# Per-head weight products of an attention kernel as 64-row tiled matmuls instead of zero-padded 128-row ones

## The chip, the cores and the metric

The kernel runs on one NeuronCore of one Trainium2 chip. The metric is device time in microseconds of one execution. The kernel before takes 453.39 us, the median of three runs (453.31 to 454.78).

## The reference, cut to what matters

Four sub-layers follow each other on x of shape (8, 256, 128), each added to its input: an attention with a time-difference kernel, a gated feed-forward layer, a causal softmax attention with 16 heads of 64, and the same feed-forward layer again. The change touches only what the third one prepares from its weights:

```
q = einsum('bsd,hda->bhsa', residual, Wq) + bq
k = einsum('bsd,hda->bhsa', residual, Wk) + bk
v = einsum('bsd,hda->bhsa', residual, Wv) + bv
scores = einsum('bhsa,bhta->bhst', q, k) * 64 ** -0.5
pattern = softmax(where(causal, scores, -1e5))
out = einsum('bsha,had->bsd', einsum('bhst,bhta->bhsa', pattern, v), Wo) + bo
```

The kernel does not form q and k. For each head it forms the 128x128 product of Wq and Wk once, and the 128x128 product of Wv and Wo once, and works with these. Each of the 32 products (16 heads, two kinds) contracts over the 64 elements of a head. The biases give a vector per head (Wk times bq) and one vector for the output (Wo times bv, summed over the heads, plus bo).

## The kernel before, in words

The rows of x are worked on in four pairs of batches (512 rows, 4 tiles of 128). A prologue brings the first pair through the first attention and the first feed-forward layer, and prepares all weights. Then a loop of 4 x 32 steps runs the softmax attention, one head and one batch a step, and the other layers of the neighbouring pairs are laid between its steps. An epilogue ends the last pair.

The order is written out by hand in the list PROLOGUE (lines 61 to 69) as triples of a job, a first tile and a count of tiles. Every engine walks the same list and does its part of each job, so each engine's queue has the order of the list and the engines wait for each other by semaphores. The jobs in the prologue are: lns0 and lns1 (layer norm on VectorE, with the power on GpSimd), lntA, lntF and lntB (transposes on TensorE, then a rounded copy xt_hi or rt_hi on ScalarE and the rest xt_lo or rt_lo on VectorE), qkv0 to qkv2, mean, vwo, mat0, mat1 and aout (the first attention), gu0 to gu2 and down (feed-forward), w0 to w7 (weight products) and wb (biases). The jobs before the loop share two PSUM banks, X and Y; a job that writes one waits until the reader before has finished (the counters x_free and y_free).

The weights lie in SBUF with two heads above each other: partitions 0 to 63 hold an even head, 64 to 127 the odd one. To contract over 64 rows with 128-row matmuls, the kernel before keeps wv1, wq1 and bq1 with both heads' columns side by side and zeros in the half that belongs to the other head. The zeros are written by VectorE (line 611) and GpSimd (lines 759, 760), and the loads of Wv (ScalarE's queue, line 488) and of Wq and bq (SyncE's queue, lines 262, 263) wait for them.

A weight job w0 to w7 (lines 378 to 391) makes four heads' products in one PSUM bank, u_ps for even and v_ps for odd job numbers. These two banks are free until the loop. TensorE runs 4 fp32 matmuls, which are 8 weight loads and 8 matmul instructions; ScalarE copies the whole bank (128x512) into the rounded part wvo_hi or m_hi (line 546); VectorE forms the rest wvo_lo or m_lo (line 718). Job wi waits for the VectorE part of job w(i-2). The job wb (lines 370 to 377) has 8 matmuls of wk against two columns of bq1 and 8 of wo against one column of bv, and ScalarE copies both results.

The first work of the loop is u_proj and v_proj (line 283 to 285 through split3), which need all of m_hi, m_lo, the first wvo_hi and wvo_lo, and rt_hi and rt_lo of lntB.

Of the kernel before, what the change touches and what calls it, by code (L numbers as in the profile page):

```python
# [21 lines left out]
P = 128  # L22
ALU = mybir.AluOpType
ACT = mybir.ActivationFunctionType
F32 = mybir.dt.float32
# [10 lines left out]
STEPS = 2 * H  # L36
GH = PAIR // D
# [44 lines left out]
WEIGHTS = [f"w{i}" for i in range(8)]  # L82
# [46 lines left out]
def build(nc, x_d, wa_d, ga_d, woa_d, boa_d, wq_d, wk_d, wv_d, wo_d, bq_d, bv_d, bo_d, wg_d, wu_d, wd_d, out_d):  # L129
# [3 lines left out]
    with ExitStack() as ctx:  # L133
# [14 lines left out]
        wq1, wv1, bq1 = sb("wq1", [P, H // 2, 2, D]), sb("wv1", [P, H // 2, 2, D]), sb("bq1", [P, 2, H // 2])  # L148
# [34 lines left out]

        u_tiles = u_ps[:].rearrange("p (b t q) -> p b t q", b=2, t=2)
# [3 lines left out]
        zeros_v, zeros_q = sem("zeros_v"), sem("zeros_q")  # L188
# [60 lines left out]
        def _(sp):  # L249
# [9 lines left out]
            sp.wait_ge(zeros_q, 2)  # L259
            for i in range(2):  # L260
                half = slice(i * A, (i + 1) * A)
                sp.dma_start(wq1[half, :, i, :], wq_d[half, :, :]).then_inc(ld_q, 16)
                sp.dma_start(bq1[half, i, :], bq_d[half, :]).then_inc(ld_q, 16)
            sp.dma_start(bv[:], bv_d).then_inc(ld_q, 16)
            sp.dma_start(bo[:], bo_d).then_inc(ld_q, 16)
# [15 lines left out]
        def _(pe):  # L281
# [15 lines left out]
            def side(job, t0, nt, at):  # L297
# [72 lines left out]
                elif job == "wb":  # L370

                    pe.wait_ge(w_lo, 8)
                    for i in range(H // 2):
                        nc.tensor.matmul(v_ps[:, 2 * i:2 * i + 2], wk[:, i, :], bq1[:, :, i], start=True, stop=True)
                    for i in range(H // 2):
                        last = nc.tensor.matmul(v_ps[:, H:H + 1], wo[:, i, :], bv[:, i:i + 1], start=(i == 0), stop=(i == H // 2 - 1))
                    last.then_inc(w_full, 1)
                elif job in WEIGHTS:

                    i = int(job[1])  # L380
                    if i == 0:
                        pe.wait_ge(ld_v, 16 * 3)
                    if i == 4:
                        pe.wait_ge(ld_q, 16 * 7)
                    if i >= 2:
                        pe.wait_ge(w_lo, i - 1)
                    left, right = (wv1, wo) if i < 4 else (wq1, wk)
                    for j in range(4):
                        h = 4 * (i % 4) + j
                        last = nc.tensor.matmul((u_ps, v_ps)[i % 2][:, j * D:(j + 1) * D], left[:, h // 2, h % 2, :], right[:, h // 2, :], start=True, stop=True)  # L390
                    last.then_inc(w_full, 1)
# [89 lines left out]
        def _(act):  # L481
            act.dma_start(wo[:], wo_d).then_inc(ld_v, 16)
            act.wait_ge(consts_in, 4)
            nc.scalar.activation(warm[:], minus_half[:, 0:1], ACT.Tanh)
            act.wait_ge(zeros_v, 1)
            for i in range(2):
                half = slice(i * A, (i + 1) * A)
                act.dma_start(wv1[half, :, i, :], wv_d[half, :, :]).then_inc(ld_v, 16)

            def side(job, t0, nt, at):  # L490
# [47 lines left out]
                elif job == "wb":  # L538
                    act.wait_ge(w_full, 9)
# [70 lines left out]
        def _(dve):  # L610
            nc.vector.memset(wv1[:], 0.0).then_inc(zeros_v, 1)

# [6 lines left out]
            def side(job, t0, nt, at):  # L619
# [93 lines left out]
                elif job in WEIGHTS:  # L713
                    i = int(job[1])
                    dve.wait_ge(w_hi, i + 1)
                    hs = slice(4 * (i % 4), 4 * (i % 4) + 4)
                    hi, lo = ((wvo_hi, wvo_lo), (m_hi, m_lo))[i // 4]
                    nc.vector.scalar_tensor_tensor(lo[:, hs, :], (u_ps, v_ps)[i % 2][:].rearrange("p (j d) -> p j d", d=D),
                                                   (1.0, SCORE_SCALE)[i // 4], hi[:, hs, :].bitcast(F32), ALU.mult, ALU.subtract).then_inc(w_lo, 1)
# [34 lines left out]
        def _(pool):  # L754
# [4 lines left out]
            nc.gpsimd.memset(bq1[:], 0.0).then_inc(zeros_q, 1)  # L759
            nc.gpsimd.memset(wq1[:], 0.0).then_inc(zeros_q, 1)  # L760
# [66 lines left out]
```

## Time and profile before

| what | us |
|---|---|
| median of three runs | 453.39 |
| lowest, highest | 453.31, 454.78 |
| span of the profiled execution | 451.1 |
| TensorE matmul busy in the span | 405.4 (90%) |
| ScalarE busy | 310.5 (69%) |
| VectorE busy | 307.7 (68%) |
| first matmul of the loop (u_proj) starts at | 58.33 |

The span runs from the first to the last recorded instruction of the one profiled execution. That execution's own time is not given beside it; the median of the runs is 2.3 us above the span. Times inside the span are counted from its start. PE is TensorE's matmuls and PEld its weight loads, DVE VectorE, ACT ScalarE, POOL GpSimd and SP SyncE; PEq and ACTq stand for what an engine's own sequencer issues. A matmul's busy time includes the time until its result is out, so matmuls that follow each other overlap in the record.

### The profile page before, as it was taken

How to read it: one execution, taken by the hardware profiler on the slowest of the kernel's cores; microseconds unless marked ns; L12 is line 12 of the kernel's file. 1: busy time of each engine (PE TensorE's matmuls, PEld its weight loads, DVE VectorE, ACT ScalarE, POOL GpSimd, SP SyncE). 2: the span in 40 equal slices, each digit the busy share in tenths (PEclk: the TensorE clock that was granted, in tenths of full speed). 3: DMA queues.
4: the chain of work that ended last, by engine and by line, in shares of the span. 5: the costliest groups of instructions: out<-in, count | busy, mean ns of one | idle time of the engine just before them, and what ended most of it. 6: DMA issues, size and time to landing. Idle time of an engine off the chain costs nothing.

```text
span 451.1 us, 8672 instructions
## 1 busy us (share of the span) xinstructions
PE 405.4 (90%) x2591; PEld 359.2 (80%) x2591; DVE 307.7 (68%) x1322; ACT 310.5 (69%) x945; POOL 34.1 (8%) x48
## 2 busy tenths in 40 slices
PE   0857688999999999999999999999999999999766
PEld 0756677878889988888899889888899898999545
DVE  4465538666878776977777858886786687766542
ACT  1443158797868897976768887876688888778420
POOL 4030100100000000200000002000000000000000
PEclk9998869999999999999999999999999999999955
DMA  8600000000000000000000000000000000000000
GB/s 221 140 1 1 1 1 1 1 1 1 2 0 2 1 1 2 1 1 11 15 1 1 1 1 1 1 1 24 2 0 2 2 0 2 2 23 2 1 1 23
DMA packets 8157, 5.68 MB, mean 13 GB/s; under 512 B 944, under 2 KB 7856, under 8 KB 8112
## 3 DMA queue, kind: packets, MB, share of 16 engines
q1 hardware_dynamic: 6912, 4.08, 3.7%
q10 hardware_dynamic: 1200, 1.05, 0.8%
q8 instruction: 22, 0.36, 0.3%
q14 instruction: 23, 0.19, 0.1%
HBM read 4.08 MB, written 1.05 MB: 11 GB/s over the span
## 4 chain that ended last, share of the span: by engine, by line
PE 75%; ACT 10%; DVE 7%; issue 4%; DMA 2%; POOL 0%; ACTq 0%; DVEq 0%
PE bank L452 11%; PE bank L283 9%; PE bank L284 9%; PE bank L285 9%; PE bank L437 9%; PE bank L361 6%; PE bank L454 5%; PE bank L427 5%; PE bank L390 2%; DVE gated L698 2%; ACT prob L571 2%; PE bank L351 2%; DMA wv<-wv_in 2%; PE bank L306 2%; ACT gate_t L537 1%
## 5 line engine op out<-in xcount | busy, mean ns | idle before, releaser
L579 ACT ACTIVATE prob_t<-bank 128x384 f32<-128x384 f32 x128 | 62.8, 490 | 22.7 <-PE bank L437 22.5
L452 PE MATMUL bank<-prob_t,v 128*128 128x256 f32 x256 | 76.5, 381 | 0.7 <-ACT o_t L604 0.7
L437 PE MATMUL bank<-ident,prob 128*128 128x128 f32 x384 | 63.8, 275 | 4.7 <-ACT prob_t L579 4.6
L571 ACT ACTIVATE prob<-neg_s,neg_max 128x256 f32<-128x256 f32 x128 | 64.3, 503 | 0.0
L569 ACT ACTIVATE prob<-neg_s,neg_max 128x128 f32<-128x128 f32 x128 | 51.5, 403 | 12.3 <-DVE neg_max L737 12.0
L735 DVE CUSTOM_DVE_ANT_0 neg_s<-bank,mask 128x128 f32<-128x128 f32 x128 | 36.7, 287 | 33.8 <-PE bank L285 33.8
L437 PEld LDWEIGHTS bank<-ident,prob 128*128 128x128 f32 x384 | 45.4, 140 | 15.1 <-DVE prob L746 5.0
L454 PEld LDWEIGHTS bank<-prob_t,v 128*128 128x128 f32 x256 | 48.5, 190 | 6.7
L737 DVE CUSTOM_DVE_ANT_0 neg_s<-bank,mask 128x256 f32<-128x256 f32 x128 | 53.7, 420 | 0.0
L427 PE MATMUL bank<-rt,u 128*128 128x128 f32 x256 | 49.8, 276 | 0.8 <-DVE neg_max L737 0.8
L454 PE MATMUL bank<-prob_t,v 128*128 128x128 f32 x256 | 49.1, 274 | 0.0
L452 PEld LDWEIGHTS bank<-prob_t,v 128*128 128x128 f32 x256 | 42.9, 190 | 7.2 <-issue 1.9
L553 ACT ACTIVATE u<-bank,u_bias 128x256 f32<-128x256 f32 x64 | 30.1, 470 | 25.6 <-PE bank L285 25.5
L283 PE MATMUL bank<-rt_hi,u_hi 128*128 128x256 f32 x128 | 46.7, 364 | 0.0
L746 DVE TENSOR_SCALAR prob<-prob,row_inv 128x256 f32<-128x256 f32 x128 | 45.5, 355 | 0.0
L561 ACT ACTIVATE v<-bank 128x512 f32<-128x512 f32 x64 | 38.3, 598 | 10.1 <-PE bank L285 9.3
L427 PEld LDWEIGHTS bank<-rt,u 128*128 128x128 f32 x256 | 41.1, 192 | 3.6 <-issue 1.0
L772 POOL TENSOR_TENSOR rstd<-var,minus_half 128x4 f32<-128x4 f32 (+1 forms) x20 | 17.8, 888 | 313.4 <-DVE var L636 313.4
L745 DVE TENSOR_SCALAR prob<-prob,row_inv 128x128 f32<-128x128 f32 x128 | 37.5, 293 | 4.6
L723 DVE SCALAR_TENSOR_TENSOR u_lo<-bank,u_bias,u_hi 128x256 fp32r<-128x256 f32 x64 | 30.8, 481 | 13.6 <-ACT u_hi L554 13.5
L285 PE MATMUL bank<-rt_lo,u_hi 128*128 128x256 f32 x128 | 36.0, 281 | 0.0
L284 PE MATMUL bank<-rt_hi,u_lo 128*128 128x256 f32 x128 | 35.9, 280 | 0.0
(117 smaller groups left out, 879.4 us busy)
## 6 DMA issues: line engine op xcount, KB each, us to landing
x<-x_in SPq DMA_DIRECT2D x3, 256.0 KB, 7.0
out<-x SPq DMA_DIRECT2D x3, 256.0 KB, 2.3
wo<-wo_in ACTq DMA_DIRECT2D x1, 512.0 KB, 4.3
wv<-wv_in ACTq DMA_DIRECT2D x2, 256.0 KB, 6.8
wk<-wk_in SPq DMA_DIRECT2D x1, 512.0 KB, 8.1
wq<-wq_in SPq DMA_DIRECT2D x2, 256.0 KB, 8.6
x<-x_in SPq DMA_DIRECT2D x2, 128.0 KB, 4.3
out<-x SPq DMA_DIRECT2D x2, 128.0 KB, 1.8
```

Of the source, the lines that this page charges most:

```text
L283: nc.tensor.matmul(out, w_hi_ap, r_hi_ap, start=True, stop=False)
L284: nc.tensor.matmul(out, w_lo_ap, r_hi_ap, start=False, stop=False)
L285: return nc.tensor.matmul(out, w_hi_ap, r_lo_ap, start=False, stop=True)
L427: nc.tensor.matmul(S[:, 0:P], u[:, i, b, :], rt[:, q, t:t + P], start=True, stop=True)
L437: last = nc.tensor.transpose(pt_ps[:, j * P:(j + 1) * P], prob[:, k % 4, j * P:(j + 1) * P], ident[:])
L452: nc.tensor.matmul(o_ps[:, b * N:(b + 1) * N], vg[:, 2 * b, hs], prob_t[:, k % 2, 0:N], start=(step == 0), stop=False, skip_group_check=True)
L454: nc.tensor.matmul(o_ps[:, b * N + P:(b + 1) * N], vg[:, 2 * b + 1, hs], prob_t[:, k % 2, N:SC], start=False, stop=(step >= STEPS - 2), sk ...
L569: nc.scalar.activation(prob[:, q, 0:P], neg_s[:, r, 0:P], ACT.Exp, bias=neg_max[:, q, 0:1], scale=-1.0, accum_out=row_sum[:, q, 0:1])
L571: nc.scalar.activation(prob[:, q, P:SC], neg_s[:, r, P:SC], ACT.Exp, bias=neg_max[:, q, 1:2], scale=-1.0, accum_out=row_sum[:, q, 1:2]).th ...
L579: nc.scalar.activation(prob_t[:, k % 2, :], pt_ps[:, 0:SC], ACT.Copy).then_inc(pt_sb, 1)
L737: nc.vector.tensor_tensor_reduce(out=neg_s[:, r, P:SC], in0=s_ps[r][:, P:SC], in1=mask[:], scale=-1.0, scalar=3e38, op0=ALU.add, op1=ALU.m ...
L746: nc.vector.tensor_scalar(prob[:, q, P:SC], prob[:, q, P:SC], row_inv[:, q, 1:2], None, ALU.mult).then_inc(p_norm, 1)
```

## The change: what it does

The products use 64-row slices of the weights, the even head in partitions 0 to 63 and the odd one in 64 to 127. The two go to different PSUM banks: even heads to u_ps, odd heads to v_ps. One job now makes eight heads in both banks, with 8 matmuls of 64 rows (alternating between the halves), two copies on ScalarE and two rests on VectorE. Both of a job's copies wait for its last matmul. There are four such jobs, w0 to w3. The job wb has 16 matmuls of 64 rows and one column for the bq part and two copies of its result. The zero memsets and the waits for them are gone; Wv is issued on ScalarE's queue right behind Wo as one load of 512 KB, Wq as one load of 512 KB.

In the list, w0 stays where it was, and w1, w2 and w3 stand where w2, w4 and w6 stood. The places of the former w1, w3, w5 and w7 are empty.

```diff
+HALVES = (slice(0, A), slice(A, P))
-    ("lntA", 2, 2), ("w1", 0, 0), ("qkv1", 0, 2), ("qkv0", 2, 2), ("qkv1", 2, 2), ("qkv2", 0, 2), ("mean", 0, 2), ("w2", 0, 0),
-    ("vwo", 0, 2), ("qkv2", 2, 2), ("mat0", 0, 2), ("mean", 2, 2), ("mat1", 0, 2), ("w3", 0, 0), ("vwo", 2, 2), ("mat0", 2, 2),
-    ("aout", 0, 2), ("mat1", 2, 2), ("w4", 0, 0), ("lns0", 0, 2), ("lns1", 0, 2), ("aout", 2, 2), ("lns0", 2, 2),
-    ("lntF", 0, 2), ("gu0", 0, 2), ("lns1", 2, 2), ("w5", 0, 0), ("lntF", 2, 2), ("gu0", 2, 2), ("w6", 0, 0), ("gu1", 0, 2),
-    ("w7", 0, 0), ("gu2", 0, 2), ("down", 0, 2), ("lns0", 0, 2), ("gu1", 2, 2), ("gu2", 2, 2), ("down", 2, 2), ("lns0", 2, 2),
+    ("lntA", 2, 2), ("qkv1", 0, 2), ("qkv0", 2, 2), ("qkv1", 2, 2), ("qkv2", 0, 2), ("mean", 0, 2), ("w1", 0, 0),
+    ("vwo", 0, 2), ("qkv2", 2, 2), ("mat0", 0, 2), ("mean", 2, 2), ("mat1", 0, 2), ("vwo", 2, 2), ("mat0", 2, 2),
+    ("aout", 0, 2), ("mat1", 2, 2), ("w2", 0, 0), ("lns0", 0, 2), ("lns1", 0, 2), ("aout", 2, 2), ("lns0", 2, 2),
+    ("lntF", 0, 2), ("gu0", 0, 2), ("lns1", 2, 2), ("lntF", 2, 2), ("gu0", 2, 2), ("w3", 0, 0), ("gu1", 0, 2),
+    ("gu2", 0, 2), ("down", 0, 2), ("lns0", 0, 2), ("gu1", 2, 2), ("gu2", 2, 2), ("down", 2, 2), ("lns0", 2, 2),
...
-            sp.wait_ge(zeros_q, 2)
-            for i in range(2):
-                half = slice(i * A, (i + 1) * A)
-                sp.dma_start(wq1[half, :, i, :], wq_d[half, :, :]).then_inc(ld_q, 16)
-                sp.dma_start(bq1[half, i, :], bq_d[half, :]).then_inc(ld_q, 16)
-            sp.dma_start(bv[:], bv_d).then_inc(ld_q, 16)
-            sp.dma_start(bo[:], bo_d).then_inc(ld_q, 16)
+            for dst, src in ((wq, wq_d), (bq, bq_d), (bv, bv_d), (bo, bo_d)):
+                sp.dma_start(dst[:], src).then_inc(ld_q, 16)
...
-                        nc.tensor.matmul(v_ps[:, 2 * i:2 * i + 2], wk[:, i, :], bq1[:, :, i], start=True, stop=True)
+                        for half, ps in zip(HALVES, w_banks):
+                            nc.tensor.matmul(ps[:, i:i + 1], wk[half, i, :], bq[half, i:i + 1], start=True, stop=True)
...
-                    if i >= 2:
-                        pe.wait_ge(w_lo, i - 1)
-                    left, right = (wv1, wo) if i < 4 else (wq1, wk)
+                    if i:
+                        pe.wait_ge(w_lo, 2 * i)
+                    left, right = (wv, wo) if i < 2 else (wq, wk)
                     for j in range(4):
-                        h = 4 * (i % 4) + j
-                        last = nc.tensor.matmul((u_ps, v_ps)[i % 2][:, j * D:(j + 1) * D], left[:, h // 2, h % 2, :], right[:, h // 2, :], start=True, stop=True)
+                        for half, ps in zip(HALVES, w_banks):
+                            last = nc.tensor.matmul(ps[:, j * D:(j + 1) * D], left[half, 4 * (i % 2) + j, :], right[half, 4 * (i % 2) + j, :],
+                                                    start=True, stop=True)
                     last.then_inc(w_full, 1)
...
             act.dma_start(wo[:], wo_d).then_inc(ld_v, 16)
+            act.dma_start(wv[:], wv_d).then_inc(ld_v, 16)
             act.wait_ge(consts_in, 4)
             nc.scalar.activation(warm[:], minus_half[:, 0:1], ACT.Tanh)
-            act.wait_ge(zeros_v, 1)
-            for i in range(2):
-                half = slice(i * A, (i + 1) * A)
-                act.dma_start(wv1[half, :, i, :], wv_d[half, :, :]).then_inc(ld_v, 16)
...
-                    nc.scalar.activation(u_bias[:], v_ps[:, 0:H], ACT.Copy, scale=SCORE_SCALE)
+                    for e in range(2):
+                        nc.scalar.activation(u_bias[:, e:H:2], w_banks[e][:, 0:H // 2], ACT.Copy, scale=SCORE_SCALE)
...
-                    dst = (wvo_hi, m_hi)[i // 4][:, 4 * (i % 4):4 * (i % 4) + 4, :]
-                    nc.scalar.activation(dst, (u_ps, v_ps)[i % 2][:].rearrange("p (j d) -> p j d", d=D), ACT.Copy,
-                                         scale=(1.0, SCORE_SCALE)[i // 4]).then_inc(w_hi, 1)
+                    for e in range(2):
+                        dst = (wvo_hi, m_hi)[i // 2][:, 8 * (i % 2) + e:8 * (i % 2) + 8:2, :]
+                        nc.scalar.activation(dst, w_banks[e][:].rearrange("p (j d) -> p j d", d=D), ACT.Copy,
+                                             scale=(1.0, SCORE_SCALE)[i // 2]).then_inc(w_hi, 1)
...
-            nc.vector.memset(wv1[:], 0.0).then_inc(zeros_v, 1)
...
-                    dve.wait_ge(w_hi, i + 1)
...
+                    for e in range(2):
+                        dve.wait_ge(w_hi, 2 * i + e + 1)
+                        hs = slice(8 * (i % 2) + e, 8 * (i % 2) + 8, 2)
+                        nc.vector.scalar_tensor_tensor(lo[:, hs, :], w_banks[e][:].rearrange("p (j d) -> p j d", d=D),
+                                                       (1.0, SCORE_SCALE)[i // 2], hi[:, hs, :].bitcast(F32), ALU.mult, ALU.subtract).then_inc(w_lo, 1)
...
-            nc.gpsimd.memset(bq1[:], 0.0).then_inc(zeros_q, 1)
-            nc.gpsimd.memset(wq1[:], 0.0).then_inc(zeros_q, 1)
```

## Rows read from the trace of the kernel before

**Rows 1.** The page: busy us (share) and instructions; granted clock in 40 slices; a group.

```profile
PE 405.4 (90%) x2591; PEld 359.2 (80%) x2591; DVE 307.7 (68%) x1322; ACT 310.5 (69%) x945; POOL 34.1 (8%) x48
...
PEclk9998869999999999999999999999999999999955
...
L437 PE MATMUL bank<-ident,prob 128*128 128x128 f32 x384 | 63.8, 275 | 4.7 <-ACT prob_t L579 4.6
```

**Rows 2.** Windows: stretch, length, busy us (instructions) by engine, PEclk, DMA share, GB/s.

```profile
33.00:36.40 3.40, 2.99 (x14) 2.93 (x14) 1.62 (x5) 0.43 (x2) 0.70 (x1) 0.50 0.02 5
...
58.33:63.80 5.47, 5.47 (x14) 4.36 (x15) 0.48 (x1) 2.03 (x4) 0.00 (x0) 0.50 0.01 3
63.80:440.00 376.20, 359.12 (x2341) 319.29 (x2340) 274.31 (x1223) 290.27 (x900) 22.41 (x23) 0.99 0.01 3
```

**Rows 3.** Chain that ended last, 0 to 110 us: start, length, what.

```profile
3.67 7.50 DMA wv<-wv_in
...
13.29 0.33 PE bank L283
...
50.64 1.68 PE bank L374 x16
```

**Rows 4.** DMA issues of the page: count, KB each, median us to landing.

```profile
wo<-wo_in ACTq DMA_DIRECT2D x1, 512.0 KB, 4.3
wv<-wv_in ACTq DMA_DIRECT2D x2, 256.0 KB, 6.8
```

**Rows 5.** Windows of one us in the load phase.

```profile
3.00:4.00 1.00, 0.00 (x0) 0.00 (x0) 0.00 (x0) 0.00 (x0) 0.68 (x3) 1.00 1.06 421
```

**Rows 6.** Timeline, 3 to 17 us: start, us, engine, line, what, count, idle before.

```profile
3.01 1.29 ACTq L488 DMA_DIRECT2D wv<-wv_in  x2
...
5.23 0.49 DVE L631 BATCH_NORM_STATS2 stats<-x 128x6 f32<-128x128 f32 x2 [2.25 <-DMA x<-x_in]
...
12.50 0.42 DVE L658 TENSOR_TENSOR xt_lo<-bank,xt_hi 128x256 fp32r<-128x256 f32 x1
...
14.27 1.87 PE L390 MATMUL bank<-wo,wv 128*128 128x128 f32 x8
...
15.02 0.42 DVE L658 TENSOR_TENSOR xt_lo<-bank,xt_hi 128x256 fp32r<-128x256 f32 x1 [0.38 <-ACT xt_hi L497]
...
16.17 0.60 ACT L546 ACTIVATE wvo_hi<-bank 128x512 fp32r<-128x512 f32 x1 [1.19 <-PE bank L390]
...
16.67 0.56 ACT L513 ACTIVATE t_qkv<-bank,ga_bias,ga_scale 128x256 f32<-128x256 f32 x1
```

**Rows 7.** Timeline, 19 to 30 us.

```profile
19.97 1.14 PE L390 MATMUL bank<-wo,wv 128*128 128x128 f32 x8
...
24.86 0.62 POOL L786 TENSOR_SCALAR stdp<-signed 128x512 f32<-128x512 f32 x1 [1.13 <-DVE signed L687]
...
25.55 0.97 PEld L341 LDWEIGHTS bank<-vwo,stdp 128*128 128x128 f32 x8 [0.62 <-issue]
...
27.14 0.69 DVE L687 SCALAR_TENSOR_TENSOR signed<-less,expd 128x512 f32<-128x512 f32 x1
...
28.27 0.69 DVE L718 SCALAR_TENSOR_TENSOR m_lo<-bank,m_hi 128x512 fp32r<-128x512 f32 x1 [0.44 <-ACT m_hi L546]
...
28.88 0.48 DVE L631 BATCH_NORM_STATS2 stats<-x 128x6 f32<-128x128 f32 x2
```

**Rows 8.** Timeline, 35 to 44 us.

```profile
35.43 0.60 DVE L642 TENSOR_SCALAR xn<-x,mv,rstd 128x128 f32<-128x128 f32 x2
...
36.98 0.69 DVE L718 SCALAR_TENSOR_TENSOR m_lo<-bank,m_hi 128x512 fp32r<-128x512 f32 x1 [0.96 <-ACT m_hi L546]
37.59 0.41 DVE L658 TENSOR_TENSOR xt_lo<-bank,xt_hi 128x256 fp32r<-128x256 f32 x1
...
40.42 0.69 DVE L718 SCALAR_TENSOR_TENSOR m_lo<-bank,m_hi 128x512 fp32r<-128x512 f32 x1 [0.47 <-ACT m_hi L546]
...
43.59 1.42 PEld L361 LDWEIGHTS bank<-wd,hid 128*128 128x128 f32 x12 [1.35 <-DVE hid L701]
```

**Rows 9.** Timeline, 50 to 55 us.

```profile
50.48 1.84 PE L374 MATMUL bank<-bq,wk 128*128 128x2 f32 x16
...
52.03 0.60 DVE L642 TENSOR_SCALAR xn<-x,mv,rstd 128x128 f32<-128x128 f32 x2
...
54.41 0.67 PE L306 MATMUL bank<-ident,xn 128*128 128x128 f32 x2
```

More of the change, by code:

```diff
@@ L79 @@
 KINDS = {"lntA": "lnt", "lntF": "lnt", "lntB": "lnt", "gu0": "gu", "gu1": "gu", "gu2": "gu"}
-WEIGHTS = [f"w{i}" for i in range(8)]
+WEIGHTS = [f"w{i}" for i in range(4)]
 class Counts:
@@ L147, in build @@
         wk, wo, bv = sb("wk", [P, H // 2, D]), sb("wo", [P, H // 2, D]), sb("bv", [P, H // 2])
-        wq1, wv1, bq1 = sb("wq1", [P, H // 2, 2, D]), sb("wv1", [P, H // 2, 2, D]), sb("bq1", [P, 2, H // 2])
+        wq, wv, bq = sb("wq", [P, H // 2, D]), sb("wv", [P, H // 2, D]), sb("bq", [P, H // 2])
         bo = sb("bo", [P, 1])
@@ L182, in build @@
         s_ps, pt_ps, u_ps, v_ps, o_ps, X, Y = bank[0:2], bank[2], bank[3], bank[4], bank[5], bank[6], bank[7]
+        w_banks = (u_ps, v_ps)
         u_tiles = u_ps[:].rearrange("p (b t q) -> p b t q", b=2, t=2)
         ld_x0, ld_x1, ld_x, ld_o, ld_a, ld_f, ld_v, ld_q = (sem(n) for n in ("ld_x0", "ld_x1", "ld_x", "ld_o", "ld_a", "ld_f", "ld_v", "ld_q"))
-        zeros_v, zeros_q = sem("zeros_v"), sem("zeros_q")
         consts = sem("consts")
@@ L381, in side @@
                     if i == 0:
-                        pe.wait_ge(ld_v, 16 * 3)
-                    if i == 4:
-                        pe.wait_ge(ld_q, 16 * 7)
-                    if i >= 2:
-                        pe.wait_ge(w_lo, i - 1)
-                    left, right = (wv1, wo) if i < 4 else (wq1, wk)
+                        pe.wait_ge(ld_v, 16 * 2)
+                    if i == 2:
+                        pe.wait_ge(ld_q, 16 * 5)
+                    if i:
+                        pe.wait_ge(w_lo, 2 * i)
+                    left, right = (wv, wo) if i < 2 else (wq, wk)
                     for j in range(4):
-                        h = 4 * (i % 4) + j
-                        last = nc.tensor.matmul((u_ps, v_ps)[i % 2][:, j * D:(j + 1) * D], left[:, h // 2, h % 2, :], right[:, h // 2, :], start=True, stop=True)
+                        for half, ps in zip(HALVES, w_banks):
+                            last = nc.tensor.matmul(ps[:, j * D:(j + 1) * D], left[half, 4 * (i % 2) + j, :], right[half, 4 * (i % 2) + j, :],
+                                                    start=True, stop=True)
                     last.then_inc(w_full, 1)
@@ L538, in side @@
                 elif job == "wb":
-                    act.wait_ge(w_full, 9)
-                    nc.scalar.activation(u_bias[:], v_ps[:, 0:H], ACT.Copy, scale=SCORE_SCALE)
+                    act.wait_ge(w_full, 5)
+                    for e in range(2):
+                        nc.scalar.activation(u_bias[:, e:H:2], w_banks[e][:, 0:H // 2], ACT.Copy, scale=SCORE_SCALE)
                     nc.scalar.activation(o_bias[:], v_ps[:, H:H + 1], ACT.Identity, bias=bo[:]).then_inc(w_hi, 1)
@@ L714, in side @@
                     i = int(job[1])
-                    dve.wait_ge(w_hi, i + 1)
[L716 to L719, printed above, removed]
+                    hi, lo = ((wvo_hi, wvo_lo), (m_hi, m_lo))[i // 2]
+                    for e in range(2):
[3 more added lines that the diff above has]
+                                                       (1.0, SCORE_SCALE)[i // 2], hi[:, hs, :].bitcast(F32), ALU.mult, ALU.subtract).then_inc(w_lo, 1)
             def u_low(h):
```

## The prediction

> **What bounds the kernel now.** I read the page first, then windows of busy time, then the chain of waits of the first 110 us, then the timeline of the prologue. The page has TensorE busy for 90% of the span [rows 1]. The windows split this: from 63.8 to 440 us TensorE is busy 359 of 376 us, so the loop is bound by TensorE, and no line of it is in the diff [rows 2]. The change can act only by moving the moment at which the loop starts, 58.33 us, and through the clock that TensorE has there. The prologue is not bound by one engine. It is one chain that passes between VectorE, GpSimd, ScalarE and TensorE, and each weight job lies across it in the three queues.
>
> The clock matters as a second thing. The granted clock is at its lower level (0.50, which is 1.2 GHz) from about 33 to 36.4 us and again for the first 5.47 us of the loop [rows 2]. At the lower level a weight job of 8 instructions takes 1.87 us, at the upper one 1.14 us [rows 6, 7]. From the starts of these, instructions follow each other by about 0.21 and 0.12 us: 1.14 us less the 0.275 us of one 128-column matmul [rows 1] is spread over 7 intervals.
>
> **The start.** The chain of waits has 7.5 us of the load of Wv in it [rows 3], and the change issues that load at about 1.2 us in place of 3.01 [rows 6]. That looks like a gain of 1.8 us or more, but two queues join at this point. The first real matmul after w0, of qkv0, needs xt_lo, which VectorE ends at 12.50 + 0.42 = 12.92 us [rows 6]; the chain shows TensorE free of w0 at 13.29 us [rows 3]. So the wait for Wv costs only 13.29 - 12.92 = 0.37 us less a hand-over of about 0.1, say 0.25. VectorE's own chain begins at 5.23 us when the first x tiles land [rows 6] and has no long wait after that, so it moves with this landing.
>
> Here the change works against itself. x (128 KB) and Wo (512 KB, landed 4.3 us after issue at 0.7) share the 16 DMA engines, which are full at 3 to 4 us with 421 GB/s [rows 4, 5]. Before, Wv came to the engines only after that. Now it is queued directly behind Wo and keeps the engines full while the last pieces of x move. The upper bound for the delay of x is the whole of Wv at that rate, 512 KB / 421 GB/s = 1.25 us, the lower bound zero. I take a third, +0.4 us, since the two queues share and x is nearly through. The Wq load and the memsets on GpSimd have nothing waiting for them before 26 us; they count zero. So w0 itself leaves the path: -0.25 against +0.4, which is +0.15.
>
> **The former w1.** It ran 14.27 to 16.14 us, while xt_lo of the second half was ready at 15.44 [rows 6]. Without it qkv1 starts about 0.3 us earlier. Then ScalarE's copy for w1 (start to next start 0.50 us) stood ahead of the tanh at 16.67 [rows 6]. Together about -0.45 us, up to -0.7. Against that, w0 and w1 kept TensorE dense from 11 to 16 us, and the durations fall from the slow to the fast kind after w1. Without w1 TensorE is used in pieces there and may stay at the lower level for some us more. Three projections in the chain would each take 0.2 to 0.3 us longer: 0 to +0.7, I take +0.2.
>
> **The new w1 to w3.** Each has 16 loads and 16 matmuls of 64 rows where the job at that place had 8 of 128. The trace has no 64-row matmul. If even and odd halves run fully beside each other, a job takes as long as before, 1.14 us; if not at all, twice as many intervals of 0.12 us, +1.0 us. I take the first, because the two halves use different rows of the array, different partitions and different banks, and keep the second for the range. What is certain is the second copy and the second rest. ScalarE's second copy delays what stands behind it by 0.48 us (0.50 in [rows 6]).
>
> At w1 the chain goes on through ScalarE: vwo, tanh, dist, expd, then signed, stdp and aout. That aout waits for stdp, and not for the former w3, is seen in its weight load at 25.55 us, 0.07 after stdp ends at 24.86 + 0.62 = 25.48 [rows 7]. So w1 costs +0.48, and the removed w3 gives nothing: it was hidden behind this chain.
>
> At w2 (formerly w4) the next link is VectorE's layer norm: m_lo at 28.27, then stats at 28.88, 0.61 us apart [rows 7]. The second rest puts another +0.61 in front of stats. TensorE and VectorE before it, aout, its addition and signed at 27.14 [rows 7], shift as a whole.
>
> The former w5 stood ahead of lntF of the second half. xn was ready at 35.43 + 0.60 = 36.03 us, about when w5 ended, so its TensorE time was hidden, but its rest at 36.98 pushed xt_lo to 37.59 [rows 8]. Without it xt_lo follows ScalarE's copy at about 37.1: -0.47.
>
> The former w6 and w7 become w3. Before, w6's rest at 40.42 and w7's each stood ahead of one feed-forward step, up to down's weights at 43.59 [rows 8]. Now both rests stand ahead of gu1 and none ahead of gu2. Following it with the same durations (copies 0.48 apart, rests 0.61 apart, second half of the job's rest ends near 41.75 instead of 41.1, then gated, hid, gate, gated, hid) down starts at about 43.9: +0.3.
>
> **wb.** xn is ready at 52.03 + 0.60 = 52.63, but lntB starts at 54.41 [rows 9], so wb is on the path. Its bq part has 16 instructions of 0.105 us in the chain, 1.68 us [rows 3]; it gets 32. With halves side by side this stays 1.68, without it grows by 1.68. The second copy of the bias is short and mostly beside lntB's transposes: +0.1.
>
> **Switching.** Going from 128-row to 64-row matmuls may not be pipelined: the matmul before has to leave the array, 0.275 - 0.12 = 0.16 us more than the usual interval [rows 1, 7]. On the path are the entries of w1, w2, w3 and wb and the exit of wb, five, so 0 to 0.8; I take 0.5. The Trainium skill (TensorEngine Tiling (Array Packing), Tiling Modes, Key Properties) says that changing the tiling mode drains TensorE; by it the term is the full 0.8, and no row here shows it. The same section says that tiles can execute weight loads and matmuls in parallel, which speaks for no growth of the jobs; no row shows that either.
>
> **The sum.** 0.15 - 0.45 + 0.2 + 0.48 + 0.61 - 0.47 + 0.3 + 0.1 + 0.5 = +1.4 us at the first u_proj. Two clock terms remain. Around 34 us the former w5 filled TensorE at the lower level (2.99 of 3.40 us busy [rows 2]) and the clock rose right behind it. Without it the clock may rise later, over gu0, w3 and gu1: 0 to +1.3, I take +0.3. At the loop's entry TensorE runs dense at the lower level for 5.47 us. Work there counts half, so a later start inside it loses less: down to -1.0, and if the clock rises later too, up to +1.5; I take -0.1. That is +1.6 us on the span of 451.1, thus 452.7; the median of the runs is 2.3 us above the span, so 453.4 + 1.6 = 455.0 us.
>
> **Rivals.**
> Halves not side by side. For it: before, weight loads alone already set the pace, since the wb matmuls of 2 columns follow each other by 0.105 us, nearly the 0.12 us of those with 128 [rows 3, 7]; if the loads of both halves pass one after the other, nothing overlaps and padding was free. Against it: different rows. Price: three jobs by +0.95 and wb by +1.68, 4.5 us, on top of the 1.6, less about 0.6 for the later entry into the slow stretch: 458.9 us. An overlap in part lies between.
>
> Clock comes up before the loop's dense part, the case on the faster side. The place is the stretch from wb to 63.8 us. Its 5.47 us at the lower level would take 2.7 at the upper one [rows 2], and transposes and the wo part of wb another 0.6. If the shifted work leaves TensorE fast there, 3.3 us come back: +1.6 - 3.3 = -1.7, 451.7 us. It decides once the lower level lasts less than 2.5 us of dense loop work (half of 5.47 - 2.5, about 1.5 us, is then saved). For it: the three runs of one kernel differ by 1.4 us, as a moved clock change would make them. Against it: the change takes TensorE work out of the prologue, and wb keeps its matmuls of one column, behind which the clock fell.
>
> That the change does not do what it says, the padding gone but all costs hidden, is the part of my own case that ends near 453.4.
>
> **How the numbers follow.** No change is what lies within 0.3%, 1.36 us, of 453.39. My case has 0.48: by its own bounds 452.9 to 457.0, of which I give 0.26 slower, 0.20 same, 0.02 faster. Halves one after the other, wholly or in part, 0.34: 0.33 slower, 0.01 same. The clock case 0.18: 0.13 faster, 0.05 same. That makes 0.15 faster, 0.26 same, 0.59 slower. The range goes from the clock case's 451.9 to 459.4, just past the second case.
>
> **What would show it.** Right: u_proj's first matmul at about 59.7 to 60 us; stats of x at about 5.6; qkv0 without a wait for Wv and w0 over long before it; each w1 to w3 about 1.1 to 1.3 us on TensorE at the upper level; two copies 0.48 apart behind each. Wrong: 16 matmuls of a job in over 1.8 us at the upper level (second case); x landing at 5.2 and a chain that does not stretch behind w2 (then my sum is too high by 1); a granted clock of 1.00 before the loop's fifth microsecond. Loop work from 64 to 440 us that changes by more than its shift would say the reasoning misses something altogether.

## The result and the profile after

The changed kernel takes 465.64 us (median of 4 runs, 464.09 to 468.05) against 454.08 us for the kernel before beside it: ratio 1.0243, 95% interval [1.0188, 1.0298]. It is 11.6 us slower. The direction was forecast, the size was not: 455.0 us, range to 459.4. Here and below the ratios are taken from fast runs alone, and four of the ten runs of e9 (462.4 to 462.9 us) are left out of its numbers as slow ones.

The experiments ran in four groups, each beside runs of the kernel before (453.9 to 454.7 us). Where two experiments are compared, the intervals of their ratios say whether the difference is more than noise.

The page of the changed kernel (its first row and the granted clock in 40 slices, as in [rows 1]) and four windows of it (columns as in [rows 2]):

```profile
PE 413.5 (89%) x2607; PEld 364.7 (79%) x2607; DVE 306.0 (66%) x1321; ACT 310.9 (67%) x946; POOL 32.5 (7%) x46
...
PEclk9975658999999999999999999999999999999955
```

```profile
25.80:32.70 6.90, 6.06 (x32) 5.35 (x32) 3.23 (x8) 2.63 (x6) 1.93 (x3) 0.52 0.01 2
...
36.00:46.40 10.40, 6.24 (x30) 4.86 (x30) 4.56 (x13) 2.51 (x6) 0.70 (x1) 0.52 0.00 1
...
49.70:69.20 19.50, 14.96 (x79) 13.09 (x78) 6.31 (x22) 2.48 (x9) 1.43 (x2) 0.50 0.00 1
...
73.30:451.40 378.10, 360.61 (x2346) 320.21 (x2344) 274.49 (x1224) 291.18 (x901) 22.37 (x23) 0.98 0.01 3
```

The loop starts at 69.20 us instead of 58.33, 10.87 us later, and from there to the end of its span of 462.3 us the changed kernel needs 393.1 us, against 392.8 us before, which is the same. So the loss lies ahead of the loop. There the granted clock is at its lower level (0.50, 1.2 GHz) in three long stretches, about 36 us of the time from 25.8 to 69.2. Before, it was low from 33 to 36.4 us [rows 2] and from 53.5 us on (0.50 up to the loop's start), together 8.2 us ahead of the loop.

What this did to the chain of waits is seen by putting its pieces beside each other (start, length, what). The kernel before:

```profile
25.59 1.12 PE bank L341 x8
26.71 0.91 PE bank L390 x8
...
43.60 1.62 PE bank L361 x12
...
49.04 1.60 PE bank L361 x12
50.64 1.68 PE bank L374 x16
52.33 2.22 PE bank L376 x16
```

The changed kernel (L337 is aout, L387 the weight jobs w1, w2, w3, L357 down, L371 and L373 the two parts of wb):

```profile
20.44 1.12 PE bank L387 x16
...
26.48 2.05 PE bank L337 x8
28.53 2.03 PE bank L387 x16
...
42.52 2.03 PE bank L387 x16
...
48.76 2.30 PE bank L357 x12
...
55.48 2.93 PE bank L357 x12
58.41 3.51 PE bank L371 x32
61.91 3.50 PE bank L373 x16
```

aout is +0.93 us, w2 and w3 +1.12 each (the jobs at their places took 0.91 before), the two downs +0.68 and +1.33, wb +1.83 and +1.28: 8.3 of the 10.87 us. Four of these seven pieces have the same instructions as before. A weight job of 16 instructions takes 1.12 us at w1, at the upper level, and 2.03 at w2: the halves do run beside each other, and the clock made the difference. For wb the same is seen in e15 below, where its 32 instructions of 64 rows took 1.95 us at the upper level, against 3.51 here.

The single steps, in the timeline of the changed kernel:

```profile
5.10 0.49 DVE L626 BATCH_NORM_STATS2 stats<-x 128x6 f32<-128x128 f32 x2 [5.10 <-DMA x<-x_in]
...
8.25 2.08 PE L387 MATMUL bank<-wo,wv 64*128 64x128 f32 x16
...
20.37 1.16 PE L387 MATMUL bank<-wo,wv 64*128 64x128 f32 x16
...
28.46 1.79 PEld L387 LDWEIGHTS bank<-wk,wq 64*128 64x128 f32 x16 [0.22 <-issue]
...
31.22 1.29 DVE L714 SCALAR_TENSOR_TENSOR m_lo<-bank,m_hi 128x512 fp32r<-128x512 f32 x2 [1.63 <-ACT m_hi L543]
...
32.42 0.47 DVE L626 BATCH_NORM_STATS2 stats<-x 128x6 f32<-128x128 f32 x2
...
40.75 0.42 DVE L653 TENSOR_TENSOR xt_lo<-bank,xt_hi 128x256 fp32r<-128x256 f32 x1 [1.20 <-ACT xt_hi L492]
```

x lands at 5.10 us (5.23 before [rows 6]); w0 is over at 10.3, long before qkv0. The 16 instructions of w1 take 1.16 us as the 8 did [rows 7]. Rests to stats is now 1.20 us (31.22 to 32.42), 0.61 before [rows 7]. Ahead of the weight loads of w2 there is 0.22 us of idle time that waits for nothing; between gu0 and w5 of the kernel before, at the same level, there is none.

One caution in reading PEclk: it says 1.00 from the start of both kernels, but w0 takes 2.08 us there, the duration of the lower level. The half-job kernel e4 below shows 1.00 up to its loop too, while all its weight jobs last as long as at the lower level. So the column can't be trusted ahead of its first change, and the durations have to be read instead.

Read this way, the first rise came later as well. The projections (qkv0 to qkv2) fall to the shorter duration at 16.1 us in the kernel before; in the changed kernel they still have the longer one at 18.3 us:

```profile
16.10 0.28 PE L284 MATMUL bank<-xt_hi,wa_lo 128*128 128x256 f32 x1
```

```profile
18.06 0.41 PE L280 MATMUL bank<-xt_hi,wa_lo 128*128 128x256 f32 x1
18.27 0.41 PE L281 MATMUL bank<-xt_lo,wa_hi 128*128 128x256 f32 x1
```

### The profile page after: what moved, and what is told of

It reads as the page before. It is cut to its first block, busy times and chain, and to the rows that moved or that the text cites. A ratio compares the mean times of both kernels' runs of the same rounds, so it can differ in the third digit from the quotient of the medians.

```text
span 462.3 us, 8699 instructions
## 1 busy us (share of the span) xinstructions
PE 413.5 (89%) x2607; PEld 364.7 (79%) x2607; DVE 306.0 (66%) x1321; ACT 310.9 (67%) x946; POOL 32.5 (7%) x46
## 4 chain that ended last, share of the span: by engine, by line
PE 73%; ACT 10%; DVE 9%; issue 5%; DMA 1%; POOL 1%; ACTq 0%; DVEq 0%
PE bank L450 10%; PE bank L279 9%; PE bank L280 9%; PE bank L281 9%; PE bank L435 8%; PE bank L357 6%; PE bank L452 5%; PE bank L425 5%; DVE gated L693 2%; PE bank L347 2%; ACT prob L568 2%; PE bank L302 2%; ACT gate_t L532 2%; PE bank L337 2%; PE bank L387 1%
## 5 line engine op out<-in xcount | busy, mean ns | idle before, releaser
L425 PE MATMUL bank<-rt,u 128*128 128x128 f32 x256 | 49.7, 276 | 0.8 <-DVE neg_max L733 0.8
L741 DVE TENSOR_SCALAR prob<-prob,row_inv 128x128 f32<-128x128 f32 x128 | 38.6, 301 | 4.6
```

The lines of the kernel that those rows point to most:

```text
L425: nc.tensor.matmul(S[:, 0:P], u[:, i, b, :], rt[:, q, t:t + P], start=True, stop=True)
```

## The experiments

**Fill the empty places.** The changed kernel with TensorE work added where w1, w3, w5 and w7 stood (e1: all four places, 128 rows; e2: the same with 64-row pairs; e8: only w1's; e14: only the last three).

```diff
+                elif job == "F":
+                    for j in range(4):
+                        nc.tensor.matmul(o_ps[:, j * D:(j + 1) * D], wo[:, j, :], wo[:, j + 4, :], start=True, stop=True)
```

> The changed kernel with four idle 128-row fp32 matmuls (Wo against Wo, into a bank free until the loop, result unused) at each of the four places in the order where w1, w3, w5 and w7 stood before. Theory 1 (the change took TensorE work out of the gaps, so the granted clock fell): the clock stays at 1.00 over most of 16 to 53 us as before, u_proj starts at 58.5 to 61 us instead of 69.2, time 453.5 to 457. Theory 2 (the 64-row matmuls themselves let the clock fall): the low stretches from 26 us stay, time 462 to 467. Theory 3 (the doubled copies and rests behind each job cost it): nothing gained, and the fillers' own 1 to 2 us each come on top, 465 to 470.

Measured 458.99 us, ratio 1.0096 [1.0056, 1.0136]. More work for TensorE, 6.6 us less time. It is 2 us above what theory 1 named, so theory 1 is not the whole. In the profiled execution (456.4 us) u_proj starts at 61.40 us.

```diff
+                        for half, ps in zip(HALVES, (o_ps, s_ps[0])):
+                            nc.tensor.matmul(ps[:, j * D:(j + 1) * D], wo[half, j, :], wo[half, j + 4, :], start=True, stop=True)
```

> As the run with 128-row fillers, but each filler is eight 64-row matmuls, the two halves alternating into two banks, of the same length on TensorE (16 instructions). Theory 1: any dense TensorE work holds the clock, same time as with the 128-row fillers within 1 us, 453.5 to 457. Theory 2: 64-row matmuls count for less, the clock stays low as in the changed kernel, 463 to 468, at least 5 us over the 128-row fillers. Theory 3: as theory 1 of no help, 465 to 470.

Measured 460.62 us, 1.0114 [1.0080, 1.0148]: between the ranges of theories 1 and 2, and not told apart from the 128-row fillers. Pairs of 64 rows hold the clock too; whether quite as well is not shown.

> The changed kernel with the 128-row filler only where the former w1 stood. Of the about 6 us that four fillers brought (465.6 to 459.0), this tells the share of the first rise of the clock. If the fall at 26 us and the later ones come from the other three gaps: 462 to 466. If the first rise decides what follows: 457 to 461.

Measured 465.28 us, 1.0225 [1.0163, 1.0286]: nothing gained, as the first case named (462 to 466). Its profile adds something: with this one filler the clock did not fall at 25.8 us, though w3's place was still empty. It fell at 34.7 us instead and then stayed at 0.50 to 72 us, which cost as much.

> The changed kernel with 128-row fillers at the places of the former w3, w5 and w7, none at w1. With e8_fill_w1_only, which brought nothing: the three places carry the gain, 457 to 461. If it takes all four together, since the first rise comes late without w1: 462 to 466.

Measured 461.01 us, 1.0144 [1.0107, 1.0180]: at the edge of the first range (457 to 461). The three places carry 4.6 of the 6.6 us, though the interval overlaps that of all four. The profiled execution also has the late first rise that the second case named: by the durations TensorE was at the lower level until about 29.5 us, and PEclk says 1.00 there. With a filler at w1's place as well (e1) the rise is at 16.3 us. Below are e14's filler at w3's place, at the lower level, and its first aout, at the upper one:

```profile
27.69 2.06 PE L377 MATMUL bank<-wo 128*128 128x128 f32 x8
...
30.39 1.10 PE L337 MATMUL bank<-vwo,stdp 128*128 128x128 f32 x8
```

In e1's profiled execution the clock stayed at 1.00 where it had first fallen in the changed kernel (25.8 us) and from 44 to 57 us, but it was low from 33.3 to 43.5 us all the same, and again from 57 us:

```profile
26.00:36.00 10.00, 4.98 (x39) 4.33 (x40) 5.62 (x19) 3.38 (x8) 2.83 (x5) 0.86 0.01 2
36.00:46.00 10.00, 8.38 (x47) 6.96 (x45) 4.96 (x12) 2.52 (x7) 0.00 (x0) 0.63 0.00 0
46.00:56.00 10.00, 7.23 (x69) 6.34 (x69) 5.41 (x21) 0.77 (x2) 1.43 (x2) 1.00 0.01 2
```

**Take TensorE work out of the kernel before**, and nothing else (e13).

```diff
-                    for j in range(4):
+                    for j in range(1 if i in (3, 5, 7) else 4):
```

> The kernel before with one matmul of four in each of w3, w5 and w7; 9 of the 32 products are not computed, all copies, rests and waits stay. TensorE has 18 instruction pairs less and nothing else changes. Clock theory: less work is slower, the clock falls near 26 us and is low more often, 457 to 464. Latency theory: up to 0.7 us a job saved where it is on the path, w5 and w7, 451.5 to 453.5.

Measured 458.96 us, 1.0118 [1.0075, 1.0162]: less work, 4.6 us slower. The order, the copies, the rests and the waits are those of the kernel before, and only 9 of the 32 products are left out. So this shows the mechanism without any part of the change. In the profiled execution the loop starts at 62.45 us instead of 58.33 and takes 393.4 us from there. One detail of the expectation missed: the clock fell at about 31 us and not near 26. First the windows of the kernel before, then those of this one, with two of its thinned jobs:

```profile
36.00:46.00 10.00, 6.77 (x46) 5.53 (x46) 5.49 (x14) 3.11 (x7) 0.00 (x0) 0.98 0.00 0
46.00:56.00 10.00, 7.45 (x54) 6.48 (x53) 4.93 (x19) 1.76 (x6) 1.43 (x2) 0.88 0.00 1
```

```profile
36.00:46.00 10.00, 7.06 (x36) 6.12 (x36) 4.75 (x12) 2.62 (x6) 0.00 (x0) 0.73 0.01 2
46.00:56.00 10.00, 8.38 (x41) 7.81 (x40) 4.81 (x19) 0.77 (x2) 1.43 (x2) 0.61 0.00 1
```

```profile
22.91 0.47 PE L390 MATMUL bank<-wo,wv 128*128 128x128 f32 x2
...
33.76 0.63 PE L390 MATMUL bank<-wk,wq 128*128 128x128 f32 x2
```

The granted clock is lower (0.73 and 0.61 against 0.98 and 0.88), and TensorE is busier with fewer instructions.

**Order apart from tiling.** e3: the padded 128-row matmuls of the kernel before, in the changed order (four jobs of eight heads).

```diff
+                    for e in range(2):
+                        for j in range(4):
+                            h = 8 * (i % 2) + 4 * e + j
+                            last = nc.tensor.matmul((u_ps, v_ps)[e][:, j * D:(j + 1) * D], left[:, h // 2, h % 2, :], right[:, h // 2, :], start=True, stop=True)
```

> The kernel before with its padded 128-row matmuls and memsets, but in the changed kernel's order: four jobs of eight heads, each 8 matmuls of 128 rows into both banks, then two copies and two rests. TensorE work is that of before, only lumped. Theory 1: the gaps at the four empty places remain, but each job is twice as long (about 2 us), so the clock falls in part: 456 to 463. Theory 2: with 128-row work the clock holds as before; the lumping alone costs the 1 to 2 us of my prediction plus 3 us of longer jobs, 456 to 459. Theory 3: all of the change's cost is the lumping, 464 or more.

Measured 470.42 us, 1.0331 [1.0271, 1.0391], worse than theories 1 and 2 allowed and within what theory 3 named. The new order costs 16 us with padded matmuls, and tiling takes 4.8 of them away: a merged job took 3.62 us at the lower level, against 2.03 tiled. Lumping alone, with all TensorE work kept, brings the fall (at about 27 us). So the amount of TensorE work alone doesn't decide; where it stands counts as well. The longer jobs also cost by themselves: 1.59 us each at the lower level, 4.8 us for the three behind w0, which is as much as tiling saves in this order.

```profile
45.78 3.62 PE L391 MATMUL bank<-wk,wq 128*128 128x128 f32 x16
```

**How much of the array works.** e4: eight jobs at the old places, each four 64-row matmuls of one half. e7: the same with the other half of the rows busy beside each.

```diff
+                    e, g = i % 2, i // 2 % 2
+                    half = HALVES[e]
+                    for j in range(4):
+                        last = nc.tensor.matmul(w_banks[e][:, j * D:(j + 1) * D], left[half, 4 * g + j, :], right[half, 4 * g + j, :],
+                                                start=True, stop=True)
```

> The kernel before's order with eight jobs, one copy and one rest each, but each job is four 64-row matmuls of one half only (even heads into u_ps, odd heads into v_ps), without padding or memsets, and wb as in the changed kernel. Instructions, job lengths and places are those of before. Theory 1: the clock holds as before, 452 to 455. Theory 2: 64-row work counts for less and the clock falls, 458 to 466. Theory 3: nothing is doubled, 452 to 455.

Measured 470.99 us, 1.0327 [1.0262, 1.0392], 5 us above the highest range named.

```diff
+                        nc.tensor.matmul((o_ps, s_ps[0])[e][:, j * D:(j + 1) * D], left[HALVES[1 - e], 4 * g + j, :], right[HALVES[1 - e], 4 * g + j, :],
+                                         start=True, stop=True)
```

> The half-job kernel (eight jobs of four 64-row matmuls of one half, 471 us) with each matmul preceded by one in the other half of the rows into a bank free until the loop, result unused. The halves overlap, so job lengths stay 2.07 us at the lower clock. Theory R (what holds the clock is how much of the array works, 64 rows alone count for half): the clock rises about 16 to 20 us as in the kernel before, 454 to 459. Theory G (the clock was low because w0 now runs alone at 8 us and leaves a gap up to 12.8 us, rows do not matter): the clock stays low, 466 to 472.

Measured 460.06 us, 1.0128 [1.0049, 1.0207]: eleven us faster by adding matmuls. First a job of the half kernel (the third of eight, all eight took 2.07 us), then two matmuls of the other, from the two halves:

```profile
21.96 2.07 PE L388 MATMUL bank<-wo,wv 64*128 64x128 f32 x8
```

```profile
26.04 0.37 PE L388 MATMUL bank<-wo,wv 64*128 64x128 f32 x1
26.05 0.37 PE L390 MATMUL bank<-wo,wv 64*128 64x128 f32 x1
```

They start 0.01 us apart, so the halves are truly beside each other. In the half kernel's profile no job ever had the shorter duration; by the durations its clock came up only inside the loop. In the other the projections have the shorter duration from 18.0 us. That is what theory R said, though 460.06 us lies just above its range: 64 rows working alone hold the clock much worse than both halves together. The added matmuls double the number of instructions as well as the rows at work, and the two are not told apart by this pair alone; the kernel before, with 128 rows and no more instructions than e4, held the clock.

**No lumping.** e9: tiled pairs in eight small jobs at the old places, half as long on TensorE. e10: every pair computed twice.

```diff
+                    for j in range(2):
+                        for e, half in enumerate(HALVES):
+                            last = nc.tensor.matmul(w_sets[i % 2][e][:, j * D:(j + 1) * D], left[half, 2 * (i % 4) + j, :], right[half, 2 * (i % 4) + j, :],
                                                     start=True, stop=True)
```

> The change without its lumping: 64-row pairs in both halves, no padding or memsets, but eight jobs at the places of the kernel before, each two pairs into two banks (a second set of banks free until the loop alternates), two copies and two rests of 128x256 instead of one of 128x512. TensorE's job is half as long as before (8 instructions, about 0.6 us at the upper clock). If the missing TensorE work in the gaps is what costs: the clock is low for much of the prologue, 460 to 467. If it is the lumping (gaps at four empty places, doubled copies behind one job) that costs: 452 to 456.

Measured 458.36 us (six runs), 1.0075 [1.0037, 1.0113]: between the two ranges named.

> As e9_tiled_small, with every pair computed once more into banks free until the loop, result unused, ahead of the real ones: TensorE's jobs have the length and the use of rows of the kernel before. Clock theory: at least 3 us faster than e9_tiled_small although TensorE does twice as much, and within 3 us of before, 453 to 458. Rival (latency of jobs, copies and rests): 0.5 us a job slower than e9_tiled_small, by 2 to 4 us.

Measured 458.21 us, 1.0079 [1.0048, 1.0110]. The old places are worth 7.3 us to the tiled kernel. Doubling the pairs changed 0.2 us: it neither gained the 3 us of the clock theory nor cost the 2 to 4 us of its rival. So here the amount of work in a job made no difference that can be seen, unlike in e13. Both theories missed; gain and cost may have met, which these runs don't show.

**Two suspects for the rest.** e15: the kernel before with wb tiled as in the change. e16: e1 with w0 held back.

```diff
+                        for half, ps in ((slice(0, A), u_ps), (slice(A, P), v_ps)):
+                            nc.tensor.matmul(ps[:, i:i + 1], wk[half, i, :], bq[half, i:i + 1], start=True, stop=True)
```

```diff
                         pe.wait_ge(ld_v, 16 * 2)
+                        pe.wait_ge(ln_var, 2)
```

> The kernel before with the bq part of wb alone as in the change: 16 matmuls of 64 rows and one column in two banks, two copies. The two halves overlap in the changed kernel's trace (32 pairs in 3.5 us at the lower clock), so 0 to +0.5 us on 454. If the rest of 4 us is in wb, 456.5 to 459.

Measured 455.09 us, 1.0005 [0.9975, 1.0036]: no cost that stands out of the noise (at most 1.6 us), where the second case asked for 2.5 or more. The 32 instructions of 64 rows take no longer to speak of than the 16 before (1.84 us [rows 9]):

```profile
50.45 1.95 PE L377 MATMUL bank<-bq,wk 64*128 64x1 f32 x32
```

> The changed kernel with four 128-row fillers and w0 held back until VectorE has the second half's variance at about 11 us, where w0 ran in the kernel before. If the early w0 with TensorE idle from 10.3 to 12.9 us behind it is the rest, 454 to 457. If not, w0 ends against qkv0 and costs 0 to 0.5 us: 458.5 to 460.

Measured 457.33 us, 1.0075 [1.0030, 1.0119]: between the two ranges, and not told apart from e1, whose interval overlaps.

**Hold the clock.** e5: the kernel before with wb split and early in a bank of its own. e6: with fillers in the three waits before u_proj. e11: two more fillers. e12: the same for the changed kernel.

The order of e11 against the kernel before:

```diff
-    ("aout", 0, 2), ("mat1", 2, 2), ("w4", 0, 0), ("lns0", 0, 2), ("lns1", 0, 2), ("aout", 2, 2), ("lns0", 2, 2),
-    ("lntF", 0, 2), ("gu0", 0, 2), ("lns1", 2, 2), ("w5", 0, 0), ("lntF", 2, 2), ("gu0", 2, 2), ("w6", 0, 0), ("gu1", 0, 2),
+    ("aout", 0, 2), ("mat1", 2, 2), ("w4", 0, 0), ("F4", 0, 0), ("lns0", 0, 2), ("lns1", 0, 2), ("aout", 2, 2), ("lns0", 2, 2),
+    ("wbo", 0, 0), ("lntF", 0, 2), ("F4", 0, 0), ("gu0", 0, 2), ("lns1", 2, 2), ("w5", 0, 0), ("lntF", 2, 2), ("wbq", 0, 0), ("gu0", 2, 2), ("w6", 0, 0), ("gu1", 0, 2),
...
-    ("lns1", 0, 2), ("lns1", 2, 2), ("wb", 0, 0), ("lntB", 0, 2), ("lntB", 2, 2),
+    ("lns1", 0, 2), ("lns1", 2, 2), ("F7", 0, 0), ("lntB", 0, 2), ("F5", 0, 0), ("lntB", 2, 2), ("F5", 0, 0),
```

Here wbo and wbq are the two parts of wb, and F7, F5 and F4 are fillers of so many matmuls. e5 moves the two parts of wb and has no fillers. e6 adds F7 and the two F5, e11 the two F4 as well. e12 is the changed kernel with the moves and fillers of e6 and the four fillers of e1; it lacks e11's F4 behind the job at w4's place and behind lntF.

> The kernel before with wb split in two (Wo times bv, Wk times bq), written to a bank that is free until the loop and placed in two gaps where TensorE waits: ahead of lntF and ahead of gu0 of the second half. Nothing else changes. [...] 450 to 453. Rival (the place of wb does not matter, its time returns in the gaps): 453 to 455.

Measured 453.02 us, 0.9960 [0.9929, 0.9992], where the two ranges meet; it doesn't decide between them.

> As the run before it, and 128-row filler matmuls (Wo against Wo, result unused) in the three waits between down and u_proj: 7, 5 and 5 fp32 matmuls. If the price of the loop's entry is the clock, it stays at 1.00 through the entry and the 5.5 us of dense work at 0.50 in the kernel before take 2.8: 447 to 450.5. If the fillers come in at the lower clock they take twice as long and delay the transposes: 453 to 456.

Measured 450.94 us, 0.9911 [0.9873, 0.9948], 0.4 us above the clock case's range. In the profiled execution the clock stayed at 1.00 from 52 us into the loop.

> The kernel before with wb split and early, fillers in the three waits before u_proj (450.9 us), and two more fillers of four matmuls, behind w4 and behind lntF of the first half, where the clock still fell at 36.4 us. Clock theory: no low stretch between the first rise and the epilogue, 448.5 to 450.5. Rival (these fillers delay the transposes and gu0 by as much as they save): 450.5 to 453.

Measured 449.98 us, 0.9899 [0.9856, 0.9942]: faster than both kernels. Its windows, and the first matmul of the loop:

```profile
26.00:36.00 10.00, 8.66 (x74) 8.18 (x73) 7.21 (x23) 3.81 (x8) 3.36 (x6) 1.00 0.01 2
...
46.00:56.00 10.00, 7.87 (x48) 7.11 (x48) 5.17 (x20) 0.77 (x2) 1.43 (x2) 0.83 0.01 2
56.00:66.00 10.00, 9.58 (x60) 8.04 (x58) 3.63 (x17) 6.12 (x17) 0.00 (x0) 1.00 0.00 0
```

```profile
59.23 0.47 PE L283 MATMUL bank<-rt_hi,m_hi 128*128 128x512 f32 x1 [0.18 <-DVE rt_lo L665]
```

The loop starts 0.9 us later than before and still the whole is faster, since its first matmuls run at the upper level (0.47 us, before 0.77 in the same place): from u_proj to the end it takes 390.7 us, before 392.8. The time lies in the range of the clock theory, but the clock was not held quite everywhere, against the expectation: 0.83 from 46 to 56 us.

> The changed kernel with the same treatment: four fillers at the empty places, wb split and early, fillers in the three waits before u_proj. With the clock held, what is left of the change is its structure: doubled copies and rests, switching, against the removed jobs, +1.4 us in the prediction's sum. So 450.5 to 453.5, 0 to 2.5 us above e6_wb_early_fill. If the clock still falls in the middle of the prologue: 454 to 458.

Measured 456.49 us, 1.0038 [1.0012, 1.0065], inside the worse case named, 5.5 us above e6 and 6.5 above e11. In the profiled executions (453.97 us, one of the two fastest of e12, and 451.84 us, the slowest of e11) the gap is only 2.1 us. There e12's loop starts 1.3 us later than e11's, at 60.55 us and at the upper level, but the clock was less well held: it was low for 10.2 us ahead of the loop (e11: 3.4) and once more for some 3 us inside it, at 72 us.

```profile
60.55 0.47 PE L279 MATMUL bank<-rt_hi,m_hi 128*128 128x512 f32 x1 [0.18 <-DVE rt_lo L660]
```

## Why the prediction was wrong

The step that failed is the clock term of the sum. The prediction took +0.2 us (bound +0.7) for the first rise and +0.3 us (bound +1.3) around the former w5, and a net -0.1 at the loop's entry. It treated the clock as a thing of three short places. Of the former w3 it said that removing it "gives nothing: it was hidden behind this chain". That was true of its latency and left out its use. The emptied places were gaps in which the former jobs had kept TensorE at work. Without them the clock fell at 25.8 us, and with it down, aout, w2, w3, both downs and wb took 8.3 us longer. Fillers at the four empty places bring 6.6 us back, and taking work out of the former w3, w5 and w7 in the kernel before costs 4.6; that part is shown. That w3 alone did it is not shown, and e8 speaks against it: its clock did not fall there with w3's place empty.

Step by step:
- The start: w0 left the path, as forecast. The delay of x (+0.4) did not come; x landed 0.13 us earlier.
- The halves run beside each other (1.16 us for 16 instructions): right, and the second case, 458.9 us, fell. That its time lies nearer to the measured one is chance, as its mechanism did not occur.
- The switch: the forecast took 0.1 us a crossing, out of a tail of 0.16; 0.22 us idle stands ahead of the weight loads of w2, at the lower level. By the Trainium skill (TensorEngine Tiling (Array Packing), Tiling Modes) TensorE drains at a change of mode; the idle time agrees with that, and is small.
- Doubled rest at w2: +0.59 us measured, +0.61 forecast. The removed w5: xn to xt_lo went from 2.16 us [rows 8] to 1.79 (38.96 to 40.75), -0.37 at the lower clock, -0.47 forecast. So these two structural terms were about right in size.
- The first stretch, up to the first mean: forecast -0.1 (0.15 - 0.45 + 0.2), measured +0.33 (19.10 and 19.43 us on the chain). The later first rise of the clock is in this number, so it doesn't check the structural terms by themselves.
- wb: forecast +0.1, measured +3.1, from the clock: tiled in the kernel before it costs nothing that stands out of the noise, and its first part takes 1.95 us there (e15; 3.51 in the changed kernel).
- The clock case on the faster side looked at this very stretch and asked whether the clock would rise earlier. The opposite, that it would be low through all of it, was bounded at +1.5 us, with 19.5 us of low clock measured from 49.7 us to the loop and 4 us more in it.
- The range starts at 451.9 us, while the clock case it is taken from gives 451.7; nothing hangs on the slip.

What stays open: with the places filled (e1, e16) or with the old places (e9, e10) the tiled kernels still take 0.75 to 0.96% more than the kernel before, 3.4 to 4.4 us. The tiled wb is ruled out as the main part, and holding w0 back gave 1 to 1.7 us, which is within the noise. The profiled executions say where the rest lies. The table has the first matmul of the prologue with the short duration, and the time at the lower level after that, as PEclk has it:

| kernel | first rise seen at, us | low clock from there to the loop, us | loop starts at, us | from there to the end, us |
|---|---|---|---|---|
| before | 16.1 | 8.2 | 58.33 | 392.8 |
| e1, four fillers | 16.3 | 14.5 | 61.40 | 393.2 |
| e10, old places, twice | 16.8 | 15.6 | 63.02 | 391.4 |
| e9, old places | 18.3 | 18.1 | 60.25 | 392.9 |
| e14, last three fillers | about 29.5 | 14.7 | 65.65 | 393.4 |
| e13, before with less work | 15.6 | 24.5 | 62.45 | 393.4 |
| e8, filler at w1 | 17.9 | 33.9 | 68.61 | 394.2 |
| changed | 18.3 to 19.4 | 36.8 | 69.20 | 393.1 |
| e3, padded and merged | 17.7 | 40.1 | 73.83 | 391.1 |

The loop itself is the same within about 3 us in all of them. Its start broadly follows the time at the lower level, the first stretch included, and the tiled kernels with the places filled or kept still have about twice that of the kernel before behind the first rise. From before to e13 a microsecond of low clock went with 0.25 us, from before to the changed kernel with 0.38. By these two, as an estimate, e1's 6.3 us more of low clock would be 1.6 to 2.4 of its 3.1 us, which leaves 0.7 to 1.5 us for structure; the sum had +1.4. One execution of each kernel was profiled, for e1, e9 and e10 one of its fastest, and no run separates the two, so this stays argued and not shown.

## What to carry to other kernels

In a stage bound by latency, TensorE work that costs nothing on the chain may still be what keeps its clock up. Before removing or bunching it, look at the granted clock after it and price every TensorE piece behind it at both levels. Here bunching eight jobs into four cost 16 us with padded matmuls and 11.6 us with tiled ones. A few unused matmuls in the waits, with the bias job moved forward, brought the kernel before to 0.990 of its time. Look at several executions before trusting one profile of the clock: the times of one kernel differed by up to 6.5 us.

## What the runs showed of the hardware

- Two 64-row matmuls in different halves and banks start 0.01 us apart, and 16 instructions take the time of 8 whole ones (1.16 and 1.14 us).
- 64-row matmuls of one half alone leave the clock low where pairs raise it: 471.0 against 460.1 us with the same places and job lengths. Matmuls with zeros in 64 rows of their weights held it in the kernel before (1.00 from 16 to 33 us); bunched together in e3 they did not.
- In the kernel before, the clock fell at 53.5 us in the middle of wb, whose matmuls of one and two columns had run without a break for 3 us.
- Single runs of one kernel spread by up to 6.5 us (e1: 455.98 to 462.51). In e1 the time follows the mean granted clock of the run: 456.0 us at 0.959, 459.0 at 0.948, 462.4 at 0.943. It is no safe measure between kernels: e4 took 470.96 us at 0.975 and 471.63 at 0.929, and in the profile of the first the column says 1.00 through a prologue whose durations are those of the lower level.
- Going from 128-row to 64-row matmuls leaves 0.22 us without a weight load at the lower level (w2, 28.46 us), and going back as much.
